# Turning the probabilities by VectorE and DMAs instead of TensorE, with the block transpose behind the reciprocal

## The reference

```python
xn = _layernorm(x)
q = (xn @ wq).reshape(B, S, H, DQ); kv = xn @ wkv      # H = 32 heads, 128 columns each are used
scores = einsum('bqhd,bkhd->bhqk', q[..., :DN], k) * DQ ** -0.5
scores = where(causal, scores, -1e30)
probs = softmax(scores, axis=-1)                        # 256 queries x 256 keys for one batch entry and head
attn = einsum('bhqk,bkhd->bqhd', probs, v)
x = x + attn.reshape(B, S, H * DV) @ wo + ffn(xn)
```

## Time and profile before

| | |
|---|---|
| median of 3 runs | 1087.95 us (1087.87 to 1088.72) |
| span of the profiled execution | 1086.1 us |
| TensorE matmul | 1081.5 us busy, 6376 instructions |
| VectorE | 746.5 us busy, 1842 instructions |
| ScalarE | 561.8 us busy, 1690 instructions |
| GpSimd | 741.4 us busy, 1030 instructions |
| granted TensorE clock | full in all 40 slices of the span |
| DMA | 23875 packets, 54.39 MB, 50 GB/s |

### The profile page before, as it was taken

The page is one execution under the profiler, slowest core; times in us unless marked ns, Lnnn a source line. Parts: engine busy times, 40 slices in busy tenths (PEclk is TensorE's granted clock), DMA queues, the critical chain, the costliest instruction groups (busy, mean ns, idle before and its releaser), DMA issues.

```text
span 1086.1 us, 21396 instructions
## 1 busy us (share of the span) xinstructions
PE 1081.5 (100%) x6376; PEld 957.6 (88%) x6376; DVE 746.5 (69%) x1842; ACT 561.8 (52%) x1690; POOL 741.4 (68%) x1030
## 2 busy tenths in 40 slices
PE   9999999999999999999999999999999999999999
PEld 8888878998998898889888988898899889988987
DVE  7598965567767666776667666666667666676675
ACT  4445221134745555556556646654665466555663
POOL 4777567997938972977487648864795579379911
PEclk9999999999999999999999999999999999999999
DMA  5111342111200210111011101110111022001102
GB/s 174 40 59 41 105 137 68 57 37 40 79 20 20 79 40 21 40 60 39 20 59 40 39 19 59 40 39 19 60 48 49 0 60 73 25 16 57 45 1 78
DMA packets 23875, 54.39 MB, mean 50 GB/s; under 512 B 3424, under 2 KB 4000, under 8 KB 23648
## 3 DMA queue, kind: packets, MB, share of 16 engines
q1 hardware_dynamic: 23488, 52.84, 15.2%
q10 hardware_dynamic: 288, 0.52, 0.1%
HBM read 51.26 MB, written 2.10 MB: 49 GB/s over the span
## 4 chain that ended last, share of the span: by engine, by line
PE 96%; POOL 3%; DVE 1%; issue 0%; ACT 0%; POOLq 0%; DVEq 0%
PE banks L186 28%; PE banks L187 28%; PE banks L188 28%; PE banks L2074 4%; PE banks L2093 3%; PE banks L2065 3%; POOL acc L534 1%; PE banks L1315 1%; POOL form_lo L1639 0%; PE banks L1177 0%; DVE mixed L883 0%; PE banks L1365 0%; POOL form_hi L1637 0%; POOL tT_lo L540 0%; POOL wc_lo L488 0%
## 5 line engine op out<-in xcount | busy, mean ns | idle before, releaser
L1639 POOL TENSOR_TENSOR form_lo<-wqk_stage,form_hi 128x256 fp32r<-128x256 f32 x192 | 141.7, 738 | 16.0
L1693 POOL TENSOR_SCALAR vf_hi<-wvo_stage 128x512 fp32r<-128x512 f32 (+1 forms) x48 | 26.3, 547 | 168.3 <-PE banks L188 155.0
L1973 ACT ACTIVATE prob<-prob,top 128x128 f32<-128x128 f32 (+1 forms) x256 | 115.7, 460 | 15.9 <-DVE top L2002 15.7
L1979 ACT ACTIVATE prob<-prob,inv 128x128 f32<-128x128 f32 (+1 forms) x256 | 102.7, 451 | 38.5 <-DVE inv L2008 38.5
L2002 DVE CUSTOM_DVE_ANT_0 prob<-banks,mask 128x128 f32<-128x128 f32 (+1 forms) x256 | 81.3, 355 | 59.4 <-PE banks L188 46.4
L2020 DVE TENSOR_TENSOR acc<-acc,banks 128x512 f32<-128x512 f32 x129 | 86.8, 677 | 35.9 <-PE banks L188 35.7
L186 PE MATMUL banks<-tT_hi,form_hi 128*128 128x512 f32 x256 | 105.6, 412 | 0.0
L187 PE MATMUL banks<-tT_lo,form_hi 128*128 128x512 f32 x256 | 100.2, 391 | 0.0
L188 PE MATMUL banks<-tT_hi,form_lo 128*128 128x512 f32 x256 | 100.1, 391 | 0.0
L186 PE MATMUL banks<-wo_hi,oT_hi 128*128 128x512 f32 x240 | 95.9, 400 | 0.0
L188 PE MATMUL banks<-wo_hi,oT_lo 128*128 128x512 f32 x240 | 93.6, 390 | 0.0
(11 more groups left out here) (351 smaller groups left out, 3730.1 us busy)
## 6 DMA issues: line engine op xcount, KB each, us to landing
wqk_stage<-in_w_qk SPq DMA_DIRECT2D x32, 512.0 KB, 3.2
wvo_stage<-in_w_v SPq DMA_DIRECT2D x34, 256.0 KB, 2.7
wvo_stage<-in_w_o SPq DMA_DIRECT2D x32, 256.0 KB, 2.7
wd_stage<-in_w_down SPq DMA_DIRECT2D x22, 256.0 KB, 2.6
gu_stage<-in_w_gu SPq DMA_DIRECT2D x10, 512.0 KB, 3.3
out<-acc SPq DMA_DIRECT2D x7, 256.0 KB, 2.0
acc<-in_x SPq DMA_DIRECT2D x6, 256.0 KB, 6.5
tab<-in_w_comb SPq DMA_DIRECT2D x1, 1300.0 KB, 6.0
```

The lines of the kernel that those rows point to most:

```text
L1639: nc.gpsimd.tensor_tensor(form_lo[:, part], src[:, :], as_f32(form_hi[:, part]), ALU.subtract).then_inc(form_ready, 1)
L1973: ins = nc.scalar.activation(pr, pr, ACT.Exp, bias=top[:, n % 2, r:r + 1], scale=-1.0, accum_out=total[:, n % 2, r:r + 1])
L1979: ins = nc.scalar.activation(pr, pr, ACT.Copy, scale=inv[:, n % 2, r:r + 1])
```

## The change

For 116 of 128 pairs (all but the first 6 and the last 6), `T` is replaced:

- `Z`, directly behind `R` in the pair's own slot: VectorE transposes each 32x32 block of `prob` into `probT`, behind ScalarE's scaling. SP waits for it and writes `probT` to a buffer in DRAM, waits for the write, and reads it back with four DMAs that put the blocks in their places, into `pT`. 
- `H`, two slots on, ahead of `X`: ScalarE copies the high part out of `pT`, VectorE makes the low part, now from SBUF. The block of the second keys is used where it landed.
- `O` comes behind the second filler that is a product, of the second slot on; `E` behind the third.
- `prob`, `pT_hi` and `pT_lo` have one buffer each; VectorE's mask waits until the pair before has been turned, TensorE's scores wait for the mask of two pairs before.
- SP walks through the group's list too: the weight loads get places in it (`D`, `K`) between the transfers of the pairs. Fillers and GpSimd's splits are put in another order; `W` of the first two tiles of a group stand in slot 0. The short ring begins at another bank.

For the 12 other pairs TensorE turns as before (`U` is the copying of the turned blocks).

```diff
@@ with_pairs
+        steps += [("T", n) for n in turned] + [("H", n) for n in landed]
+        if not landed:
+            steps += [("U", n) for n in turned]
+        steps += [("X", p)]
+        made = 0
+        for at, step in enumerate(fill):
+            steps.append(step)
+            made += step[0] in "PQW"
+            if at == 0:
+                steps += [("R", p)] + ([("Z", p)] if p not in by_pe else [])
+            if step[0] in "PQW" and made == 2 and landed:
+                steps += [("O", p - 2)]
+            if step[0] in "PQW" and made == 3 and landed and p % 2:
+                steps += [("E", p - 2)]
@@ MIDDLE_SLOTS (slots 0 to 5)
-    [("L", 0, P5), ("P", 0, P3), ("W", 0, 2), ("L", 0, P3), ("P", 1, P1), ("W", 0, 3)],
-    [("P", 1, P6), ("P", 1, P2), ("W", 0, 4), ("L", 1, P2)],
-    [("P", 1, P7), ("W", 0, 5), ("P", 1, P4)],
-    [("L", 1, P4), ("P", 1, P5), ("W", 0, 6), ("L", 1, P5), ("W", 0, 7)],
+    [("L", 0, P5), ("P", 0, P3), ("P", 1, P1), ("L", 0, P3), ("W", 0, 0), ("W", 0, 1)],
+    [("P", 1, P6), ("W", 0, 2), ("P", 1, P2), ("W", 0, 3)],
+    [("L", 1, P2), ("P", 1, P7), ("W", 0, 4), ("P", 1, P4), ("W", 0, 5)],
+    [("L", 1, P4), ("P", 1, P5), ("W", 0, 6), ("L", 1, P5), ("W", 0, 7), ("K", 3), ("D", 2), ("D", 3)],
     [("P", 1, P3), ("Q", 0, P1), ("L", 1, P3), ("Q", 0, P6)],
     [("Q", 0, P2), ("P", 2, P1), ("M", 0, P2), ("Q", 0, P7)]]
@@ OUTER_SLOTS (slots 6 to 15, the new ones)
+    [("P", 2, P6), ("Q", 0, P4), ("P", 2, P2), ("M", 0, P4), ("D", 4), ("D", 5), ("K", 4)],
+    [("L", 2, P2), ("P", 2, P7), ("P", 2, P4), ("L", 2, P4), ("P", 2, P5), ("W", 1, 0)],
+    [("L", 2, P5), ("P", 2, P3), ("W", 1, 1), ("Q", 0, P5), ("L", 2, P3), ("Q", 1, P1)],
+    [("M", 0, P5), ("Q", 0, P3), ("P", 3, P1), ("M", 0, P3), ("Q", 1, P6), ("W", 1, 2)],
+    [("Q", 1, P2), ("P", 3, P6), ("M", 1, P2), ("Q", 1, P7), ("W", 1, 3), ("K", 5)],
+    [("P", 3, P2), ("Q", 1, P4), ("L", 3, P2), ("P", 3, P7), ("M", 1, P4), ("P", 3, P4), ("W", 1, 4), ("L", 3, P4)],
+    [("Q", 1, P5), ("W", 1, 5), ("P", 3, P5), ("M", 1, P5), ("Q", 1, P3), ("L", 3, P5)],
+    [("M", 1, P3), ("P", 3, P3), ("W", 1, 6), ("L", 3, P3), ("W", 1, 7), ("D", 6), ("D", 7)],
+    [("P", 4, P1), ("P", 4, P6), ("P", 4, P2)],
+    [("L", 4, P2), ("P", 4, P7), ("P", 4, P4), ("L", 4, P4), ("P", 4, P5)]]
@@ SP
+        def bounce_pair(g, steps, n):
+            turn = bounces(g, n)
+            sp.wait_ge(block_turned, turn + 1)
+            if n >= FIRST_BOUNCED + 2 or steps is not FIRST:
+                sp.sem_inc(wait_passed, 1)
+                sp.wait_ge(bounce_in[n % 2], landings(g, n - 2))
+            sp.dma_start(bounce[n % 2], probT[:, :]).then_inc(bounce_out, 16)
+            sp.wait_ge(bounce_out, 16 * (turn + 1))
+            sp.sem_inc(wait_passed, 1)
+            sp.wait_ge(o_done, g * PAIRS + n - 1)
+            side = P // BLOCKS
+            for c in range(BLOCKS):
+                sp.dma_start(
+                    pT[c * side:(c + 1) * side, n % 2].rearrange("j (a n) -> j a n", a=BLOCKS),
+                    bounce[n % 2][:, c * 3 * side:(c + 1) * 3 * side].rearrange("(a j) n -> j a n", a=BLOCKS),
+                ).then_inc(bounce_in[n % 2], 16)
@@ ScalarE
+                elif kind == "H":
+                    act.wait_ge(bounce_in[n % 2], landings(g, n))
+                    act.wait_ge(o_done, g * PAIRS + n)
+                    nc.scalar.activation(by_block(pT_hi[:, :]), landed(n)[:, 0:2], ACT.Copy).then_inc(pT_hi_done, 1)
@@ VectorE
                 if kind == "S":
                     dve.wait_ge(s_done, g * PAIRS + n + 1)
+                    if n and by_tensor(steps, n - 1):
+                        dve.wait_ge(t_done, turned(steps, n - 1))
+                    elif n or steps is not FIRST:
+                        dve.wait_ge(block_turned, bounces(g, n - 1) + 1)
+                elif kind == "Z":
+                    dve.wait_ge(norm_done, g * PAIRS + n + 1)
+                    if n > FIRST_BOUNCED or steps is not FIRST:
+                        dve.wait_ge(bounce_out, 16 * bounces(g, n))
+                    nc.vector.transpose(probT[:, :], prob[:, :].rearrange("p (b c n) -> p c b n", b=3,
+                                                                          c=BLOCKS)).then_inc(block_turned, 1)
+                elif kind == "H":
+                    dve.wait_ge(pT_hi_done, g * PAIRS + n + 1)
+                    nc.vector.tensor_tensor(by_block(pT_lo[:, :]), landed(n)[:, 0:2], by_block(as_f32(pT_hi[:, :])),
+                                            ALU.subtract).then_inc(pT_ready, 1)
```

More of the change, by code:

```diff
@@ L64, with with_pairs @@
 LAST_MIXES = {U2: 1, C11: 2, C11_LO: 3, C12: 4, C12_LO: 5}
-def with_pairs(slots, first=False):
+FIRST_BOUNCED, LAST_BOUNCED = 6, 10
+def with_pairs(slots, by_pe):
     steps = []
     for p, fill in enumerate(slots):
-        older = [] if first and p == 0 else [p - 1]
-        late = [p - 2] if p % 2 and not (first and p == 1) else []
-        steps += [("S", p)] + [("E", n) for n in late] + [("T", n) for n in older] + [("X", p)]
-        steps += fill[:1] + [("R", p)] + fill[1:]
-        steps += [("O", n) for n in older]
+        turned = [p - 1] if p - 1 in by_pe else []
+        landed = [p - 2] if p - 2 not in by_pe else []
+        steps += [("S", p)]
+        if not landed and p % 2 and p > 1:
+            steps += [("E", p - 2)]
[12 more added lines that the diff above has]
+            if step[0] in "PQW" and made == 3 and landed and p % 2:
+                steps += [("E", p - 2)]
+        if made < 3 and landed and p % 2:
+            steps += [("E", p - 2)]
+        if landed:
+            steps += [("U", n) for n in turned]
+        steps += [("O", n) for n in turned]
     return steps
@@ L181 @@
 TOEP_AFTER = 6
+BLOCKS = 4
 def matmul3(nc, out, w_hi, w_lo, x_hi, x_lo, first, last):
@@ L1404, in attention @@
     acc, xT_hi, xT_lo, ident, _, banks, y_done = shared
-    w_qk, w_v, w_o, mask_dram, out = ins
+    w_qk, w_v, w_o, mask_dram, bounce, out = ins
     v_hi, v_lo, v_full, oT_hi, oT_lo, wo_hi, wo_lo, v_rest = late_sb
@@ L1408, in attention @@
      wvo_stage, mask) = lasting_sb
-    prob, p_full, pT_hi, pT_lo, top, total, inv, u3v = pair_sb
+    prob, probT, pT, pT_hi, pT_lo, top, total, inv, u3v = pair_sb
     HALF_G = GH * DH // 2
@@ L1446, in attention @@
     t_done = sem("t_done")
+    block_turned = sem("block_turned")
+    bounce_out = sem("bounce_out")
+    bounce_in = [sem(f"bounce_in{i}") for i in range(2)]
     pT_hi_done = sem("pT_hi_done")
@@ L1534, in turn_bank @@
         ring = LONG if long else SHORT
-        return banks[:, ring[(taken.index(step) - (len(taken) if steps is FIRST else own)) % len(ring)]]
+        at = taken.index(step) - (len(taken) if steps is FIRST else own) + (0 if long else SHORT_FROM)
+        return banks[:, ring[at % len(ring)]]
     def o_part(steps, n):
@@ L2073, in group @@
                         part = slice(block * P, (block + 1) * P)
-                        ins = nc.tensor.transpose(banks[:, S + n % 2, part], prob[:, n % 2, part], ident[:, :])
+                        ins = nc.tensor.transpose(banks[:, S + n % 2, part], prob[:, part], ident[:, :])
                     ins.then_inc(t_done, 1)
@@ L2089, in group @@
                     d = slice(h * DH, (h + 1) * DH)
-                    matmul3(nc, banks[:, O, cols], v_hi[:, b, d], v_lo[:, b, d], pT_hi[:, n % 2], pT_lo[:, n % 2],
+                    matmul3(nc, banks[:, O, cols], v_hi[:, b, d], v_lo[:, b, d], pT_hi[:, :], pT_lo[:, :],
                             True, False)
-                    ins = nc.tensor.matmul(banks[:, O, cols.start + P:cols.stop], v_full[:, b, d], p_full[:, n % 2],
+                    ins = nc.tensor.matmul(banks[:, O, cols.start + P:cols.stop], v_full[:, b, d], second_keys(n),
                                            start=False, stop=True)
```

90 lines of the change are left out of this document (51 added, 39 removed).

## The result

The changed kernel takes 1230.3 us (median of 4 runs, 1228.3 to 1231.5) against 1088.1 us before on the same chip: a ratio of 1.130, 95% interval 1.129 to 1.132. It is 142 us slower. The forecast was 1098, with 1128 as the upper end.

What follows compares the result with a forecast made beforehand. It took TensorE to bound the kernel before and VectorE after: 6 x (106.2 - 104.5) = +10.2 us for the loop, 0 for the other 20 pairs, on a median of 1087.95, gives 1098.2 us, range 1062 to 1128.

Steps and rivals of the forecast that it cites:

- TensorE's gain of 0.33 us a pair: TensorE without a pair's three transposes: 0.33 us back each, 38.3 us for 116 pairs, the most the change can gain.
- Z at 0.47 us: VectorE's block transpose of 128x384, with no row of its own: 0.47 us, ends 0.364 and 0.69.
- The chain mask to Z's end, 3.17 us: VectorE from a pair's mask to Z's end, one filler included: 3.17 us, 50.7 us for 16 chains a turn.
- The sum of 105.2 us for VectorE's turn: VectorE's time for one loop turn of 16 pairs, work plus waits, as if TensorE's products were always ready: 105.2 us.
- The turn as the larger of two sums: Loop turn taken from VectorE's 105.2 us, above TensorE's 99.2, plus about 1 us for starving: 106.2 against today's 104.5.
- I cost these moves at nothing: SP's moved value and weight loads and the later split of output weights: no cost, covered by GpSimd's waits.
- The jump, 2.5 us: VectorE standing at a turn's first mask: hidden before, counted at 2.5 us a turn once there is no slack.
- H's contention: H's low part with two SBUF operands beside GpSimd: 0.28 us more each, 1.2 us a turn left after hiding.
- The transfers: DRAM write and four reads per pair on SP's queue: 5.7 us from Z's end, hidden with 1 us to spare.
- TensorE stays the bound: Rival, faster: VectorE's turn stays below 104.5 us; 1049.7 us with TensorE bounding, 1067 halfway; chance 0.34.
- transfers late: Rival, slower: landing exceeds 5.7 + 1 us and holds H; about 1120, 1153 us at worst; chance 0.13.
- VectorE as the bound: The forecast's own case: VectorE the new bound, turn longer than before; range 1090 to 1122 us; chance 0.44.

Runs made afterwards that it cites:

- order_only: Kernel before with the changed kernel's new order, splits, loads and late O and E, but TensorE turning all pairs, no Z, H or transfers: 1180.2 us, ratio 1.085.
- order_z: Kernel before with the new order and TensorE's turning, plus the block transpose on VectorE for 116 pairs, its result unused, no transfers: 1232.2 us, ratio 1.132.
- after: The changed kernel itself, with the whole change against the kernel before: 1230.3 us, ratio 1.130.
- before_z: Kernel before in its old order, with VectorE's block transpose added behind the reciprocal for the same 116 pairs, result unused: 1114.4 us, ratio 1.024.

## Why the prediction was wrong, step by step

- **What bounds the kernel before: right, and read too loosely.** TensorE was at 100% without gaps. The prediction concluded that "the other three have slack", from busy shares of 69, 52 and 68%. That slack is an average. In order_only the same VectorE work stands at other places, and TensorE waits for it.
- **TensorE's gain of 0.33 us a pair: not refuted, and not seen.** TensorE's busy time from order_z to after fell by 32.7 us for 116 pairs, 0.28 each, at nearly the same mean clock (0.970 and 0.961).
- **Z at 0.47 us: right.** Its record has 579 ns in the mean, but the next operation starts 0.50 us behind its start. The Trainium skill (VectorE: DVE Perf Modes, The three transpose paths), whose 311 ns for 128x128 bf16 had been scaled to an estimate of 0.93 us, was not the better guide: this fp32 shape is far quicker than that estimate.
- **The chain mask to Z's end, 3.17 us: too small.** It was read from one slot and taken for all 16. Here it is 3.32 us, from 635.37 to the next operation's start, VectorE in order of time in slot 2 of the changed kernel, one of its shortest:

```profile
635.37 0.28 DVE L2089 CUSTOM_DVE_ANT_0 prob<-banks,mask 128x128 f32<-128x128 f32 x1
...
638.19 0.58 DVE L2113 STREAM_TRANSPOSE probT<-prob 128x384 f32<-128x384 f32 x1 [0.96 <-ACT prob L2062]
638.69 0.65 DVE L1859 TENSOR_TENSOR u<-u,banks 128x512 f32<-128x512 f32 x1
```

From the mask's start to Z's start the loop's 96 pairs take 3.18 us in the mean, 2.8 to 4.3 by slot. The prediction had 2.70, and 4.0 us more a turn for evacuations ahead of the scaling, which makes 2.95.
- **VectorE's wait in front of Z, 0.8 to 1.0 us: nearly right** (0.96 here; 124.5 us in 115 places, 1.08 in the mean).
- **The sum of 105.2 us for VectorE's turn: 9 us too small.** Without its waits for TensorE, VectorE's turn is 114.3 us in the changed kernel (125.6 - 11.3). The excess lies in its waits for ScalarE: besides the chains above, low parts wait 8.1 us a turn for their high part, where 4.0 were forecast. In the old order, with Z alone, the turn is 107.8 us (before_z); that this is near 105.2 is chance, since VectorE waits 7.5 us of it for TensorE.
- **The turn as the larger of two sums, with "about 1 us more" for waits: this is the step that failed.** The prediction added up VectorE's turn "as if TensorE always had its products ready", took it because it was larger than TensorE's 99.2, and allowed about 1 us for starving. Measured, both engines wait, in turn. VectorE has 81.3 us of work in a turn, 28.6 of waiting for ScalarE, 3.0 at the jump and 11.3 of waiting for TensorE (gaps under 0.15 us and one wait for a write make up the rest of 125.6); TensorE is busy 107.3 and waits 18.3 for VectorE. The sum counts how much each engine has to do. It does not follow for each low part how long after its product it is done, and which step of TensorE is next to need it. So the new places of O, E and the fillers, which change just that, entered only by VectorE's load, and order_only shows that they cost 92 us by themselves, 50 of them with O and E at their old places. For W(1,0) it could have been read off the diff: E(5) comes after the slot's third product, which is the step just ahead of W(1,0), and the earlier trace rows have prices of what is queued in front (k_full 0.38 and kT_hi 0.59 on ScalarE, a low part of 512 columns 0.68 on VectorE).
- **"I cost these moves at nothing": not refuted.** This was said of the loads and splits. In order_only TensorE waits 1.5 us for GpSimd's parts. They were not run alone.
- **The jump, 2.5 us "with no slack it counts": right in kind, too small.** In the changed kernel VectorE stands 3.3 to 4.0 us there, and writing out the loop brings 35 us, 5.8 a turn. TensorE's idle time falls by 26 us and its busy time by 10, so the pause and a part of the half-clock stretches behind it are both in that.
- **H's contention: right in kind, the operation's price too high.** Mean 594 against 421 ns is 0.17 us (0.28 forecast, between 0 and 0.41). The 1.2 us a turn forecast are 7 us for the six, as measured, but the measurement has 5 us of play. The rule of the Trainium skill (SBUF — State Buffer, Who interferes with whom), that such an operation and a GpSimd instruction that reads SBUF exclude each other, bears on it: the trace agrees in direction, with a tail up to 1.5 us, while about half of the operations are untouched (minimum 419, median 496).
- **The granted clock: missing.** The sum took TensorE's rate as fixed. In the changed kernel TensorE works 70 us at half the clock, in and behind pauses, which costs up to 35 us.
- **The transfers: right, hidden.** 1.9 + 1.9 us to land (2.0 + 2.0 assumed, from the earlier trace rows); SP needs 0.43 us for each of the four reads (0.5 assumed). From Z's end to the last landing it is 5.4 us in the median (5.7 forecast).
- **Rivals.** "TensorE stays the bound" did not come, and neither did "transfers late"; nor was the forecast's own case, VectorE as the bound, what happened. That it is slower at all was forecast from VectorE's load, and that part, 26 us in before_z, is real; two thirds of the loss have another cause, so the sign owes something to luck. The upper end of 1128 took in only these mechanisms; a price for the new order itself was in no rival, although the change moves nearly every step of the loop.

## What to carry to other kernels

When an edit reorders work among engines that hand tiles to each other, the sums per engine are only a lower bound: write down for each product when its evacuation is done on each queue and which step of the busiest engine comes next, above all where a consumer moves directly behind its producer. A wait put into an engine's queue costs what stands behind it, so Z with 122 us of waiting in front of it cost 26 us in an order with distance between producer and use, and with 117 us of waiting 52 in one without. The step that needs a result need not read it: a product that waits for its bank is one too. Ask of any TensorE pause of some us what it does to the granted clock, and run the new order with the old operations first: it is the cheapest test of a reordering.

## What the runs showed of the hardware

- A block transpose of 128x384 fp32 on VectorE takes 579 ns by its record, and 0.50 us from its start to the next operation's.
- Behind TensorE's pauses of 3.77 and 5.55 us shown above, matmuls of 512 columns start 0.42 us apart, and 0.23 us apart before and later. The granted clock is half in these stretches: at 620 to 625 us, behind the jump, it is 0.50 for the whole window.
- At the loop's jump VectorE stands 3.3 to 4.0 us with nothing to wait for, where it was 2.5 to 2.8 before. Why it is longer was not tested.
- VectorE's subtraction of 256 columns with both operands in SBUF takes 419 to 425 ns when no GpSimd instruction runs beside its first 0.4 us, and up to 1523 ns otherwise; with one operand in PSUM it takes 416 to 425.
- Reads of 48 KB in pieces of 384 bytes land in 1.9 us, no later than a write of 192 KB.
